# Three score banks and one shared work bank in a fused attention and Fourier mixer kernel

## The reference

```python
def _L0_conv_ref(x, w_qkv, w_o):
    qkv = x.reshape(8, 1024, 192) @ w_qkv          # 12 heads of 16
    attn = softmax(q @ k.T * 16 ** -0.5)
    return (attn @ v) @ w_o
def _L1_conv_ref(x, w1, b1, w2, b2, bias_w, bias_b):
    bias = x @ bias_w.T + bias_b
    xf = rfftn(x, axes=(1, 2), norm='ortho')       # 4 blocks of 48 channels
    r1, i1 = relu(complex product of xf with w1, plus b1)
    r2 = r1 @ w2[0] - i1 @ w2[1] + b2[0]
    i2 = r2 @ w2[1] + i1 @ w2[0] + b2[1]
    return irfftn(complex(r2, i2), norm='ortho') + bias
x = x + _L0_conv_ref(_gn(x), ...)                  # _gn: group norm over 32 groups
x = x + _L1_conv_ref(_gn(x), ...)
```

## Time and profile before

| | |
|---|---|
| median of three runs | 1710.0 us |
| lowest and highest | 1698.99 and 1712.88 us |
| the profiled execution, its time | 1708.25 us |
| its span, first to last instruction | 1706.4 us |
| PE, DVE, ACT busy | 94%, 73%, 57% of the span |
| mean granted clock of TensorE | 0.946 of full speed |

### The profile page before, as it was taken

The page is one execution under the profiler, slowest core; times in us unless marked ns, Lnnn a source line. Parts: engine busy times, 40 slices in busy tenths (PEclk is TensorE's granted clock), DMA queues, the critical chain, the costliest instruction groups (busy, mean ns, idle before and its releaser), DMA issues.

```text
span 1706.4 us, 28124 instructions
## 1 busy us (share of the span) xinstructions
PE 1604.6 (94%) x8580; PEld 732.8 (43%) x8580; DVE 1240.1 (73%) x2189; ACT 970.9 (57%) x1825; POOL 180.4 (11%) x249
## 2 busy tenths in 40 slices
PE   8999999999999989999999989999999998999878
PEld 4443434344544444344443444444443444433345
DVE  4887888777778877878767767787878787875022
ACT  2266676666566665666556655666655665655401
POOL 2000001300102001300003001030013000120010
PEclk8599999999899999999989998999999999987899
DMA  5402013214404224034122243032230442111123
GB/s 121 69 20 45 18 30 82 44 41 83 101 2 73 52 46 100 17 69 83 47 57 42 44 84 95 8 64 53 53 81 9 77 83 63 22 26 26 41 62 77
DMA packets 96908, 94.19 MB, mean 55 GB/s; under 512 B 26096, under 2 KB 78192, under 8 KB 96752
## 3 DMA queue, kind: packets, MB, share of 16 engines
q1 hardware_dynamic: 96752, 92.25, 26.8%
HBM read 14.32 MB, written 6.29 MB: 12 GB/s over the span
## 4 chain that ended last, share of the span: by engine, by line
PE 62%; DVE 12%; issue 8%; SPq 8%; DMA 5%; ACT 2%; POOL 2%; DVEq 0%; POOLq 0%; ACTq 0%
PE o_acc L1125 16%; PE scores L1090 12%; PE max_tiles L1104 11%; DVE row_max L867 7%; PE prep_bank L1196 4%; PE post_bank L1148 3%; DMA o_t<-o_raw 2%; PE post_bank L1260 2%; SPq L494 2%; PE prep_bank L1148 2%; SPq L561 2%; PE post_bank L1160 2%; PE post_bank L1267 2%; SPq L524 1%; ACT probs L773 1%
## 5 line engine op out<-in xcount | busy, mean ns | idle before, releaser
L867 DVE TENSOR_REDUCE row_max<-max_tiles 128x1 f32<-128x512 f32 x1536 | 970.8, 681 | 200.5 <-PE max_tiles L1104 197.3
L773 ACT ACTIVATE probs<-scores 128x512 f32<-128x512 f32 x1536 | 836.0, 597 | 398.3 <-PE scores L1090 390.7
L1090 PE MATMUL scores<-q_stack,k_stack 50*128 50x512 f32 x1536 | 616.0, 471 | 13.9 <-ACT probs L773 13.5
L1104 PE MATMUL max_tiles<-k_stack,q_stack 48*128 48x512 f32 x1536 | 609.3, 468 | 8.1 <-DVE row_max L867 4.1
L1125 PE MATMUL o_acc<-probs,v_aug 128*32 128x512 f32 x3072 | 430.6, 634 | 17.0 <-ACT o_raw L781 16.0
L1090 PEld LDWEIGHTS scores<-q_stack,k_stack 50*128 50x128 f32 x1536 | 248.1, 190 | 334.2 <-ACT probs L773 268.6
L1104 PEld LDWEIGHTS max_tiles<-k_stack,q_stack 48*128 48x128 f32 x1536 | 256.3, 192 | 158.7 <-DVE row_max L867 109.3
L437 POOL TENSOR_TENSOR o_raw<-o_raw,inv_all 128x1024 f32<-128x1024 f32 x23 | 54.4, 2365 | 926.6 <-DVE inv_all L895 926.6
L1125 PEld LDWEIGHTS o_acc<-probs,v_aug 128*32 128x32 f32 x3072 | 61.5, 109 | 139.1 <-issue 126.9
L1196 PE MATMUL prep_bank<-xt,w_qk 96*128 96x512 f32 x172 | 85.2, 618 | 0.0
L933 DVE TENSOR_TENSOR qk_parts<-prep_bank,qk_parts 128x512 fp32r<-128x512 f32 x43 | 29.8, 692 | 54.9 <-ACT qk_parts L803 54.9
(11 more groups left out here) (218 smaller groups left out, 1094.4 us busy)
## 6 DMA issues: line engine op xcount, KB each, us to landing
q_stack<-qk_parts SPq DMA_DIRECT2D x288, 64.0 KB, 2.3
k_stack<-qk_parts SPq DMA_DIRECT2D x144, 128.0 KB, 4.1
rows_b<-rows_a SPq DMA_DIRECT2D x128, 96.0 KB, 3.2
spec_b<-spec_a SPq DMA_DIRECT2D x64, 102.0 KB, 2.3
x_in<-in_x_dram SPq DMA_DIRECT2D x8, 768.0 KB, 5.5
o_t<-o_raw SPq DMA_DIRECT2D x96, 64.0 KB, 2.5
x<-in_x_dram SPq DMA_DIRECT2D x8, 768.0 KB, 7.3
rows_b<-spec_b SPq DMA_DIRECT2D x32, 192.0 KB, 3.3
```

Of the source, the lines that this page charges most:

```text
L773: nc.scalar.activation(probs[:, GH * (s % 2) + h, :], scores[:, n % SCORE_BANKS, :], ACT.Exp, scale=SCALE).then_inc(probs_made, 1)
L867: nc.vector.tensor_reduce(row_max[:, which, m:m + 1], max_tiles[:, (TILES * g + no) % MAX_BANKS, :], AX.X, ALU.max).then_inc(max_taken, 1)
L1090: mm(scores[:, n % SCORE_BANKS, :], k_stack[rows, 2 * g + hp, P * kt:P * (kt + 1)], q_stack[rows, g, half, hp, :], start=True, stop=True). ...
L1104: mm(max_tiles[:, (TILES * g + no) % MAX_BANKS, :], q_stack[rows, g, half, hp, P * qt:P * (qt + 1)], k_stack[rows, 2 * g + hp, HALF * whic ...
```

## The change

`scores` gets a third bank. `prep_bank` and `post_bank` become one bank, `work`. A piece now waits until the piece before it on PE, of whichever chain, is taken out. The transposed maxima go to `turn_bank`, a place in the rotation of the three max banks after the first four max tiles of a half: max tiles 4 and 5 of that half wait for the tile two before instead of three, and tile 6 waits for `split_shift`. In a step the first piece stands after score tile 1 and before the weighted sum on PE, after exponentials 0 and 1 on ACT, and after max tiles 0 and 1 on DVE. The setup stages of image 0 move to other steps. SP's and POOL's orders stay.

```diff
-SCORE_BANKS, MAX_BANKS = 2, 3
+TURN_AT = 4
+SCORE_BANKS, MAX_BANKS = 3, 3
...
-        prep_bank = bank("prep_bank")
-        post_bank = bank("post_bank")
+        work = bank("work")
...
+        def max_bank(unit, i):
+
+            n = 4 * (unit % HUNITS) + i
+            return max_tiles[:, (n if n < TURN_AT else n + 1) % MAX_BANKS, :]
+
+        turn_bank = max_tiles[:, TURN_AT % MAX_BANKS, :]
...
-        SETUP_AT = (10, 12, 14, 21, 27)
+        SETUP_AT = (10, 12, 14, 15, 17)
...
@@ scalar block, body @@
+                    exponentials(b, g, s, 0)
+                    exponentials(b, g, s, 1)
                     if jobs:
                         jobs[0][0](*jobs[0][1:])
-                    exponentials(b, g, s, 0)
-                    exponentials(b, g, s, 1)
...
@@ vector block, body @@
-                    if jobs:
-                        jobs[0][0](*jobs[0][1:])
                     for tile in tiles[:2]:
                         take_max(tile[0], *tile[2:])
-                    for job in jobs[1:]:
+                    for job in jobs:
                         job[0](*job[1:])
...
@@ tensor block, max_tile @@
-                after(pe, max_taken, TILES * slot + no + 1 - MAX_BANKS)
+                n = no % (2 * TILES // 4)
+                if n == TURN_AT + MAX_BANKS - 1:
+                    after(pe, shift_split, 2 * (2 * slot + half))
+                else:
+                    ago = MAX_BANKS if n < TURN_AT or n >= TURN_AT + MAX_BANKS else MAX_BANKS - 1
+                    after(pe, max_taken, TILES * slot + no + 1 - ago)
...
@@ tensor block, turn_shift @@
-                prep_taken(pe, *last_piece)
-                nc.tensor.transpose(prep_bank[0:HMAX, 0, 0:P], full_max[:, :],
+                if not over:
+
+                    pe.wait_ge(max_taken, TILES // 2 * (halves(b, g, half) + 1) + TURN_AT - MAX_BANKS + 1)
+                nc.tensor.transpose(turn_bank[0:HMAX, 0:P], full_max[:, :],
                                     ident).then_inc(shift_turned, 1)
...
@@ tensor block, body @@
+                def piece(job):
+                    nonlocal in_work
+                    if in_work:
+                        work_taken(in_work)
+                    job[0](*job[1:])
+                    in_work = ("prep" if job[0] is prep_piece else "post", *job[1:4])
+
                 for u in range(NG * STEPS):
...
-                    if jobs:
-                        jobs[0][0](*jobs[0][1:])
                     for tile in tiles[0:1]:
                         max_tile(*tile)
                     score_tile(b, g, s, 0)
                     for tile in tiles[1:2]:
                         max_tile(*tile)
                     score_tile(b, g, s, 1)
+                    for job in jobs[:1]:
+                        piece(job)
                     if s > 0:
                         pv(b, g, s - 1)
...
                     for job in jobs[1:]:
-                        job[0](*job[1:])
+                        piece(job)
```

More of the change, by code:

```diff
@@ L83 @@
 SHIFT_AT = range(STEPS // 2 - 3, NG * STEPS, STEPS // 2)
-SHIFTS_BEFORE = [sum(at < step for at in SHIFT_AT) for step in sorted(PREP_AT) for _ in PREP_AT[step]]
 ON_ACT = ("spread", "turn", "v")
@@ L372, in jobs_of @@
         def jobs_of(b, u, prep, post, prep_piece, post_piece):
[L374 to L375 removed]
+            jobs = [(prep_piece, b + 1, *p, work[:, 0, :]) for p in PREP_AT.get(u, []) if prep]
+            return jobs + [(post_piece, *p, work[:, 0, :]) for p in post_pieces(b, u, post)]
         def late_pieces(post_piece):
@@ L1375, in body @@
                     if u in shift_steps(prep):
-                        made = [p for step in PREP_AT if step <= u for p in PREP_AT[step] if prep]
-                        turn_shift(*next_half(b, u), (b + 1, *made[-1]) if made else (b, *PREP[-1]))
-                    if first and u - 1 in SETUP_AT:
-                        setup(SETUP_AT.index(u - 1))
+                        turn_shift(*next_half(b, u), u + AHEAD >= NG * STEPS and not prep)
+                    if first and u - 1 in SETUP_AT[:-1]:
+                        stage = SETUP_AT.index(u - 1)
+                        if in_work:
+                            work_taken(in_work)
+                        setup(stage)
+                        in_work = ("setup", SETUP_TAKEN[stage])
             def tail():
                 pv(NB - 1, NG - 1, STEPS - 1)
-                late_pieces(post_piece)
+                late = [p for u in sorted(LATE) for p in LATE[u]]
+                at = len(POST) - len(late)
+                for n, p in enumerate(late):
+                    post_taken(pe, NB - 2, *POST[at + n - 1])
+                    post_piece(NB - 2, *p, work[:, 0, :])
                 b = NB - 1
```

71 lines of the change are left out of this document (35 added, 36 removed).

## The result

The changed kernel takes **1799.2 us** (median of four runs, 1791.8 to 1806.5), the kernel before, on the same chip, 1704.5 (1697.5 to 1712.9). The ratio is 1.054, with an interval of 1.049 to 1.059. The forecast was 1768, 3.5% where 5.4% came. The profiled execution took 1791.8 us, 83.6 more than that of before, where the sum had 60. So the direction and the mechanism hold, and the size was too small by 24 us in the profiles and by some 37 in the medians. The time lies inside the range of 1710 to 1802, but above the 1744 to 1795 that the bounds of the main terms gave by themselves.

The account below looks back on a forecast made before the run. PE was taken to set the end, waiting for ACT only in steps without a piece. Images 1 to 6 at +11.3 us each (+68), image 0 -7, image 7 -1: +60 on 1708, about 1768 us, range 1710 to 1802.

Parts of the forecast that it names:

- The release of pair 1: Each step: second max-and-score pair (pair 1) can start 1.30 us after the third (pair 2), when DVE frees its bank.
- The restart: From pair 1's release to the weighted sum: 0.34 to 0.43 us; 0.34 was taken for steps with a piece.
- the large term: In images 1 to 6, 27 steps that begin with a large piece lose 0.30 us each: +8.1 us per image.
- the steps without a piece: In images 1 to 6, seven such steps gain 0.36 to 0.45 us, taken as 0.40: -2.8 us per image.
- shared bank: A step's second piece waits until the first is taken out: +4.0 us per image, bounds 0 to 6.
- transposed maxima: They take a max bank, so pairs behind a transpose wait 0.60 us longer: +2.6 us per image.
- absorbed waits: Existing waits, at steps 32 and 46 for DMA or regrouped rows, take in losses: -1.2 us per image.
- Image 0: No post pieces; about 26 plain steps gain 0.40 us each, ten large ones lose 0.30: -7 us in all.
- image 7: No prep pieces: plain steps -6 us, third score bank -3.5, large first pieces +3.6, pairs +2.9, maxima +2: -1 us.
- Rival 1: Faster: DVE frees the max bank before PE reaches pair 1, closing the 0.75 us bubble: about 1660 us; chance 0.10.
- Rival 2: No change: longer waits and DMA chains take in most losses: 1713 to 1732, about 1722 us; chance 0.18.
- Rival 3: Slower still: DVE is late beyond its bound, or the clock falls more often: about 1800 us; chance 0.11.

Follow-up runs that it names:

- half reductions: The changed kernel, with DVE reducing only 256 of each max tile's 512 columns: 1683.3 us, 0.986 of the kernel before.
- piece between the pairs: The changed kernel, with a step's first piece moved between pair 0 and pair 1 on PE: 1710.5 us, 1.003 of the kernel before.
- the new banks with the old order: The changed kernel, with the first piece back ahead of pair 0 on PE, ACT and DVE: 1698.3 us, 0.996 of the kernel before.
- Parting the weighted sum: The new banks with the old order, with half the weighted sum's columns moved behind pair 3 where the next step has no piece: 1728.5 us.

## Why the prediction was right in kind and too small

**The release of pair 1: right.** Forecast 1.30 us after pair 2, measured 1.32 and 1.31. The half reductions and the piece between the pairs show by runs that this wait is the loss.

**The restart: the term that was mis-sized.** For a piece step I took 0.30, "since in rows 4 pair 1 with both loads free takes the 0.34", and named 0.39 as the bound. The row of 0.34 is a pair in the middle of a burst, where loads and matmuls overlap with what ran before. A pair that starts after a wait takes the 0.43 of the earlier trace rows, which I had read and not taken. So a large-piece step (step 40) lost 0.41 in images 0, 1 and 6, and 0.48 in images 2 to 5, beyond the bound. There the released score load goes 0.08 behind the max load, as these loads of an image 2 step without pieces show:

```profile
643.26 0.18 PEld L1094 LDWEIGHTS scores<-q_stack,k_stack 50*128 50x128 f32 x1 [0.84 <-ACT probs L779]
...
644.57 0.18 PEld L1113 LDWEIGHTS max_tiles<-k_stack,q_stack 48*128 48x128 f32 x1 [0.76 <-DVE row_max L873]
644.65 0.18 PEld L1094 LDWEIGHTS scores<-q_stack,k_stack 50*128 50x128 f32 x1
```

In step 44 of image 1 both go at 432.01. Images 2 to 5 share one loop in the program, the others are written out; that the loop is the reason is an inference from where it occurs. With 27 steps an image, 0.48 in place of 0.30 is +4.9 us in each of four images, and 0.41 is +3.0 in the other two: 25 us over six.

**The rest of an image: right as a sum.** Leaving out six steps whose length swings with the clock and DMA (0, 8 to 10, 45, 47; together 32.1 before and 32.0 after), an image went from 163.9 to 180.8 us (sums of the medians by step), +16.9, and with the six it is +16.8, where I had +11.3. At 0.48 a step the large term takes 13.0 of it and the steps without pieces give back 2.0, so turn, mean, shared bank, transposed maxima and absorbed waits come to 5.8; I had 0.6 + 2.6 + 4.0 - 1.2 = 6.0. That it agrees so well is in part luck, since by steps it is less good. The transposed maxima cost the forecast 0.60 as a wait (1.91 against 1.90). `mix1` steps lost 0.41, where 0.30 + 0.20 stood, and step 28, which begins with a `dfth` piece, stands in none of my lists and lost 0.48. Two-piece steps lost more than I gave where DVE has other work ahead of the first piece. In step 29 it joins maxima first (1.41 lost, 1.30 given), step 38 went from 5.26 to 6.59, and step 23 from 4.63 to 6.01, with 0.40 given. There, in image 1, the weighted sum starts at 333.28:

```profile
332.49 1.32 DVE L901 STREAM_SHUFFLE inv_all<-inv_all 128x1024 f32<-128x1024 f32 x1
...
333.69 1.29 DVE L873 TENSOR_REDUCE row_max<-max_tiles 128x1 f32<-128x512 f32 x2
...
334.88 0.56 DVE L966 COPY rows_a<-work 128x384 f32<-128x384 f32 x1
335.49 0.30 PEld L1248 LDWEIGHTS work<-tok_n,cst 128*128 128x128 f32 x2 [2.06 <-DVE rows_a L966]
```

DVE is still at `spread_inverse` of the step before, then reduces, then takes the first piece, and the second starts 1.2 us after the sum is through.

**Steps without a piece: nearly.** 0.35 gained in the images written out, 0.28 in the others (forecast 0.36 to 0.45), for the same restart.

**Absorbed waits.** The step that ends in 32 became 0.75 shorter (4.19 to 3.44), so the DMA wait of `mix1` 0 did take in the burst's cost (forecast: 0.9 of wait against 0.30). PE's idle time before `mix1` pieces for that DMA fell from 8.7 us to 0.4 in the list of waits.

**Image 0 and image 7: wrong both ways.** Image 0 came out at +1.5 us, not -7, and image 7 at -17.8, not -1. In image 7 the kernel before has a stretch in which `mix1` steps took 6.47 us against 3.73 in image 1. Its granted clock there is 0.51 (1541 to 1562 us), that of the changed kernel in the same steps 1.00, and of the other twelve traces one has a single step as slow there (6.47 in step 32). So this is read as the clock's doing in one execution and no gain of the change. For image 0 my terms, -10.4 + 3 + 1 + 1, add up to -5.4 and not to the -7 that I carried on. Its plain steps gained 0.35 as they should. Steps 1 and 2 took 2.0 us more, at a clock of 0.79 from 76 to 90 us (0.97 before), and where setup stages moved, steps 15 to 17 took 3.2 more and step 22 took 2.2 less; the rest is not taken apart. The two images miss by +8 and by -17, and so hide part of what images 1 to 6 cost over the forecast, 31 us in the profiles.

**The rivals.** Rival 1 asked whether DVE frees the bank 0.29 sooner. The half reductions made DVE 0.27 sooner and the kernel 1683 us, so this was the right hinge, and the kernel stood on the slow side of it. The Trainium skill, "Perfetto Trace Analysis", section "Optimization Strategy", says that consistent bubbles can mean too little PSUM for the next tile. The trace agrees in kind: the third score bank returned 0.35 of the bubble of 0.75 us, and not the whole, because another bank was next in line. Rival 2 falls, as waits took in little. Rival 3 gave 1800 us, close to what came, but its price was worked out from the clock, which was no lower; its other half, DVE late beyond the bound, is seen in two-piece steps such as 23 and 38.

## What to carry to other kernels

A piece of work between bursts is not only work: it is the time in which a slower engine frees the banks. Before you move it, ask at which tile of the burst that engine is late, and keep the piece in front of that tile; here one pair of tiles further cost 89 us of 101.

Price a new wait by a row in which the engine restarts after a wait, not by one from the middle of a burst (0.43 against 0.34 here, in some 160 steps).

With banks redistributed, time each share apart. Here the third score bank's 28 us and the 22 us paid for it nearly cancel, and the sum alone, 0.4% with an interval that reaches no change, would say that banks don't matter.

## What had not been expected of the hardware

A pair that is released after a wait costs 0.08 us more in images 2 to 5 than in the others, through the second load only, and a step without such a wait costs the same (3.83 in step 40 of the new banks with the old order, in all of images 1 to 6). The cause is not isolated. In the kernel before it was hidden: its step without a piece takes 3.09 us in both.

Fewer waits on PE went with more time at the half clock in one kernel, and not in another. Parting the weighted sum shortened each plain step from 2.74 to 2.48 us and the kernel became 1.8% slower (1728.5 against 1698.3), with the granted clock at 0.64 over a stretch of 48 us in which the kernel before had 1.00. Halving the reductions also took waits away (2.81 to 2.66 in a plain step), and its clock was 0.961, above the changed kernel's 0.956. So waits alone don't decide it.
